# Statistics, powers and normalised rows of two batches in one step, in the two outer stages of a four-layer cross-attention kernel

## The chip, the cores and the metric

The kernel runs on one core of a Trainium2 chip. A core has five engines with their own instruction streams that meet through semaphores: PE (matrix multiply, with its weight load shown as PEld), DVE (vector), ACT (activation), POOL and SP (which issues the DMAs). The metric is the device time of one launch in microseconds.

## The reference, cut to what matters

Eight batches of 128 rows and 256 columns (`x`) and a context of the same shape pass through four layers. Each layer normalises the rows, attends, adds the result and runs an MLP. The normalisation is what the change touches; it is computed 64 times in the outer stages (4 layers' inputs, outputs and MLPs, 8 batches each).

```python
def layer_norm(x, w, b):                      # L0, L2, L3; also ahead of the MLP
    mu = jnp.mean(x, axis=-1, keepdims=True)
    var = jnp.mean(jnp.square(x - mu), axis=-1, keepdims=True)
    return (x - mu) * jax.lax.rsqrt(var + 1e-5) * w + b

def rmsnorm(x, w):                            # L1's MLP
    var = jnp.mean(jnp.square(x), axis=-1, keepdims=True)
    return x * jax.lax.rsqrt(var + 1e-6) * w

x = L0(x, ctx)      # cross-attention to ctx, 16 heads of 16, then MLP
x = L1(ctx, x)      # x attends to ctx and x, masked softmax; rmsnorm ahead of its MLP
x = L2(x, ctx, ctx) # two cross-attentions, 16 heads of 128, with a bias key and value; MLP
x = L3(x, ctx)      # self-attention with a mask, cross-attention with a mask, MLP
# L3: scores = scores * mask - 10000.0 * (1.0 - mask); probs = softmax(scores)
```

## The kernel before

**Streams and stages.** The 8 batches are cut into 4 streams k = 0 to 3 of SB = 2 batches. A row tile has 128 rows on the partitions, 256 columns and two batches, `m.x(k)[:, b, :]`. Stage A computes L0 and L1, stage B the two attentions of L2 (its matmuls split into high and low parts), and stage C L2's MLP (named M2), L3's self-attention (L3s), its cross-attention (L3c) and its MLP. Stage A runs over the span from 0 to about 300 us, stage C from about 820 us to the end. Stage B is a loop and is not touched. There the statistics already have the joint form, with one power for both batches (lines 954 to 959 and L1324).

**The order.** What each outer stage does stands in a text: `ORDER_ONE` (stage A, from line 359) and `ORDER_TWO` (stage C, from line 401). Each of the five engine programs walks the same text and issues its own instructions of each step, in that order. An engine never overtakes itself, so a step's place in the text is its place in every engine's queue. The last number of a step is a PSUM bank where it has one. The steps that matter:

- `stats NAME OF K B`: DVE waits for the rows, then `bn_stats` (L829), `bn_aggr` (L831) and the sum of variance and epsilon, `ve` (L838; for L1's MLP a square and an add, L834 and L836). POOL waits for `ve` and raises it to the power −0.5, `rstd` (L1324). NAME and OF are the layer and which normalisation: `in` ahead of an attention, `mlp` ahead of an MLP, and `L1 out` for the rows that stage B takes.
- `xn NAME OF K B`: the normalised row. For L0 and L1's MLP POOL computes it (L1337, or L1335 without a mean). For the others POOL computes the shift `nb` (L1328) and ACT the row (L1126).
- `turn_in NAME OF K BANK`: PE transposes the normalised rows of both batches (L481). It waits for the row of batch SB − 1, the last.
- `scores`, `minima`, `exp`, `even`, `turn`, `weigh`, `project`: the attention of a unit (a batch of a stream, in halves). PE multiplies (L573), DVE or POOL puts the mask on (L870, L873, L1371), DVE takes the minimum (L880), ACT the exponent (L1198), DVE the sum and its reciprocal (L885, L887), POOL divides (`even`, L1377), PE transposes the weights (L583) and ACT copies them (L1174), PE weighs the values (L598) and projects (L610), and DVE adds to the rows (`project`, L901).
- `residual` (L1360) is POOL's sum of rows and a bias. `up` and `down` are the MLP's two matmuls (L489, L557).

In stage A, the key mask (`m`, L1049) is made by DVE at the first unit's scores. `stats L0 in 0 1` is followed by `parities` on DVE.

In ORDER_TWO before, the last part reads:

```text
turn 15 1, stats L3c mlp 3 0, turn_in L3c mlp 2 7, xn L3c mlp 3 0, weigh 15, up L3c 2 0 4,
project 15 7, stats L3c mlp 3 1, up L3c 2 2 5, xn L3c mlp 3 1, residual L3c mlp 3,
up L3c 2 4 7, turn_in L3c mlp 3 3, up L3c 2 6 4, up L3c 3 0 5, ...
```

Of the kernel before, what the change touches and what calls it, by code (L numbers as in the profile page):

```python
# [18 lines left out]
SB = B // NS  # L19
# [323 lines left out]
class Drains:  # L343
# [24 lines left out]
    xn L0 mlp 1 0, residual L0 mlp 0, up L0 0 6 2, project 3 3, residual L0 attn 3, stats L0 mlp 1 1, turn 4 1, scores 6, minima 6, exp 5 0, even 5 0,
    exp 5 1, weigh 4, down L0 0 0 7, down L0 0 1 2, project 4 5, exp 6 0, exp 6 1, turn_in L1 in 0 0, xn L0 mlp 1 1, turn 5 0, even 5 1, v L0 3 0 1,
    even 6 0, even 6 1, turn_in L0 mlp 1 7, turn 5 1, scores 7, minima 7, k L1 0 1 7, residual L0 mlp 1, weigh 5, turn 6 0, q L1 0 3, stats L0 mlp 2 0,  # L370
    exp 7 0, v L1 0 0 5, even 7 0, project 5 0, turn 6 1, exp 7 1, stats L0 mlp 2 1, xn L0 mlp 2 0, k L1 1 0 7, scores 8, weigh 6, turn 7 0, even 7 1,
    up L0 1 0 0, up L0 1 2 4, xn L0 mlp 2 1, minima 8, up L0 1 4 7, turn 7 1, scores 9, weigh 7, exp 8 0, up L0 1 6 7, even 8 0, minima 9, v L1 0 1 3,
    residual L1 attn 0, turn_in L0 mlp 2 1, project 6 0, exp 8 1, even 8 1, exp 9 0, even 9 0, down L0 1 0 2, stats L0 mlp 3 0, turn 8 0, down L0 1 1 7,
    exp 9 1, even 9 1, turn 8 1, scores 10, weigh 8, turn 9 0, project 7 1, stats L0 mlp 3 1, turn 9 1, minima 10, turn_in L1 in 1 7, exp 10 0, exp 10 1,
    scores 11, residual L0 mlp 2, even 10 0, even 10 1, up L0 2 0 7, up L0 2 2 4, k L1 1 1 0, minima 11, up L0 2 4 2, up L0 2 6 1, exp 11 0, exp 11 1,
# [1331 lines left out]
```

## Time and profile before

| | us |
|---|---|
| median of 3 runs | 1079.56 |
| lowest, highest | 1079.14, 1081.27 |
| the profiled execution, its time | 1081.11 |
| the profiled execution, its span | 1079.80 |

The profiled execution's span is what the rows below are times in; 1.31 us lie around it. The mean granted TensorE clock of the profiled execution is 0.998. Each row is one group of instructions, or a stretch. In a timeline a row has the start, the length, the engine, the line of the kernel, the operation, output and input, and how many instructions it holds; a bracket gives the idle time of the engine before it and what ended it.

### The profile page before, as it was taken

Reading aid. Unit: us, or ns where it says so; the run is one execution under the profiler, and the core shown is the slowest. Engines: PE = TensorE matmul, PEld = TensorE weight load, DVE = VectorE, ACT = ScalarE, POOL = GpSimd, SP = SyncE. Lnnn points to the kernel's source line nnn. Section 1 sums busy time; section 2 is a strip of 40 time slices with the busy share of each in tenths; the row PEclk is TensorE's granted clock in tenths of the full one; section 3 lists DMA queues with packets and bytes.
Section 4 is the critical chain, followed back from the end, with each engine's and each line's share of the span. In section 5 each row is a group of like instructions: output and inputs, shape, how many; then the busy total and the mean of one; then the engine's idle time right before and its main releaser. Section 6 shows DMA issues by size and latency. Waiting matters only on the chain.

```text
span 1079.8 us, 20226 instructions
## 1 busy us (share of the span) xinstructions
PE 1045.6 (97%) x7794; PEld 917.4 (85%) x7794; DVE 706.6 (65%) x1088; ACT 602.2 (56%) x1323; POOL 572.0 (53%) x618
## 2 busy tenths in 40 slices
PE   6899999999999999999999999999999999988999
PEld 5788788788888999999998999999998887866887
DVE  6888778879537556555658655655654377988840
ACT  4998887778653232223334323322226489999972
POOL 7555535455664434333466434443525378999860
PEclk9999999999999999999999999999999999999999
DMA  9200000000113222122120111101100000000000
GB/s 336 112 2 21 2 1 1 2 1 2 49 42 96 70 69 59 40 79 79 40 76 26 40 40 39 40 29 31 31 1 2 1 1 1 2 2 2 10 11 20
DMA packets 33783, 40.66 MB, mean 38 GB/s; under 512 B 2111, under 2 KB 31257, under 8 KB 32025
## 3 DMA queue, kind: packets, MB, share of 16 engines
q1 hardware_dynamic: 33689, 39.38, 11.1%
q8 instruction: 63, 1.03, 0.4%
q14 instruction: 31, 0.25, 0.1%
HBM read 38.32 MB, written 1.05 MB: 36 GB/s over the span
## 4 chain that ended last, share of the span: by engine, by line
PE 77%; POOL 9%; issue 5%; DVE 5%; ACT 4%; DMA 0%; SPq 0%; POOLq 0%; DVEq 0%; ACTq 0%
PE psum L489 14%; PE psum L663 13%; PE psum L557 10%; PE psum L677 7%; PE psum L723 7%; PE psum L583 5%; PE psum L711 5%; PE psum L691 4%; POOL C tile L1371 3%; PE psum L573 3%; PE psum L598 3%; PE psum L700 2%; PE psum L541 2%; PE psum L610 2%; POOL C tile L1377 2%
## 5 line engine op out<-in xcount | busy, mean ns | idle before, releaser
L1459 POOL TENSOR_TENSOR B tile<-B tile,B rec 128x1024 f32<-128x1024 f32 x32 | 60.7, 1897 | 207.8 <-DVE B rec L994 207.8
L1377 POOL TENSOR_TENSOR A tile<-A tile,outer rec 128x1024 f32<-128x1024 f32 x48 | 90.4, 1894 | 99.4 <-DVE outer rec L887 99.4
L1257 ACT ACTIVATE B own<-B max 128x8 f32<-128x8 f32 x32 | 6.7, 210 | 163.1 <-DVE B tile L981 163.1
L1198 ACT ACTIVATE A tile<-A tile,outer min 128x128 f32<-128x128 f32 (+1 forms) x256 | 92.1, 459 | 3.6 <-DVE outer min L880 3.5
L1126 ACT ACTIVATE B kT<-psum,B bcol 128x1024 f32<-128x1024 f32 x32 | 35.6, 1113 | 90.8 <-PE psum L663 90.8
L489 PE MATMUL psum<-A hT,weights 128*128 128x256 f32 x352 | 81.2, 381 | 2.0 <-ACT A hT L1126 2.0
L489 PE MATMUL psum<-C hT,weights 128*128 128x256 f32 x352 | 80.3, 381 | 1.3 <-DVE C tile L870 1.1
L1198 ACT ACTIVATE C tile<-C tile,outer min 128x128 f32<-128x128 f32 x256 | 77.5, 398 | 3.2 <-DVE outer min L880 3.2
L1022 DVE TENSOR_TENSOR x_all<-x_all,psum 128x512 f32<-128x512 f32 x64 | 42.6, 685 | 54.3 <-PE psum L723 54.3
L489 PEld LDWEIGHTS psum<-A hT,weights 128*128 128x128 f32 x352 | 65.2, 190 | 12.5 <-ACT A hT L1126 3.2
L489 PEld LDWEIGHTS psum<-C hT,weights 128*128 128x128 f32 x352 | 65.5, 190 | 11.3 <-issue 2.1
L677 PE MATMUL psum<-B v hi,B cT hi 128*128 128x256 f32 x256 | 74.3, 290 | 0.4 <-ACT B kT L1126 0.3
L677 PE MATMUL psum<-B v hi,B cT lo 128*128 128x256 f32 x256 | 72.4, 283 | 0.0
L677 PE MATMUL psum<-B v lo,B cT hi 128*128 128x256 f32 x256 | 72.4, 283 | 0.0
L802 DVE TENSOR_SCALAR B qT<-psum,B bcol 128x1024 f32<-128x1024 f32 x32 | 41.1, 1283 | 47.3 <-PE psum L663 47.3
L1324 POOL TENSOR_TENSOR outer rstd<-outer ve,half 128x1 f32<-128x1 f32 x64 | 36.0, 565 | 67.5 <-DVE outer ve L838 55.5
L1377 POOL TENSOR_TENSOR C tile<-C tile,outer rec 128x1024 f32<-128x1024 f32 x32 | 60.5, 1897 | 10.6 <-DVE outer rec L887 10.4
L873 DVE TENSOR_TENSOR A tile<-m,psum 128x1024 f32<-128x1024 f32 x48 | 56.4, 1216 | 13.9 <-PE psum L573 13.8
L1174 ACT COPY A PT<-psum 128x512 f32<-128x512 f32 x96 | 51.5, 593 | 24.4 <-PE psum L583 24.3
L711 PEld LDWEIGHTS psum<-B PT,B v 128*128 128x128 f32 x512 | 61.4, 191 | 3.6 <-ACT B PT L1266 1.5
L711 PE MATMUL psum<-B PT,B v 128*128 128x128 f32 x512 | 62.1, 275 | 1.1 <-ACT B PT L1266 1.1
L885 DVE TENSOR_REDUCE outer sum<-A tile 128x4 f32<-128x1024 f32 (+1 forms) x48 | 57.9, 1207 | 7.6 <-ACT A tile L1198 7.5
(197 smaller groups left out, 3113.6 us busy)
## 6 DMA issues: line engine op xcount, KB each, us to landing
weights<-in_weights_c SPq DMA_DIRECT2D x6, 1024.0 KB, 6.9
raw<-in_wq SPq DMA_DIRECT2D x32, 128.0 KB, 2.7
raw<-in_wk SPq DMA_DIRECT2D x32, 128.0 KB, 2.8
raw<-in_wv SPq DMA_DIRECT2D x16, 256.0 KB, 2.7
raw<-in_wo SPq DMA_DIRECT2D x16, 256.0 KB, 2.8
weights<-in_weights_a SPq DMA_DIRECT2D x1, 3072.0 KB, 21.7
weights<-in_weights_a SPq DMA_DIRECT2D x1, 2048.0 KB, 11.3
wide<-in_bias_v SPq DMA_DIRECT2D x2, 1024.0 KB, 10.6
```

Source lines behind the costliest of these rows:

```text
L489: i = pe.matmul(bank(k)[:, n * T:(n + 1) * T], wt[:, c, (o + n) * P:(o + n + 1) * P], src[:, c, :], start=c == 0, stop=c == C - 1)
L557: i = pe.matmul(bank(z)[:, 0:D], part.aT(k)[:, c, b * P:(b + 1) * P], w2[:, c, :], start=c == 0, stop=c == FC - 1)
L583: i = pe.transpose(bank(4 + half)[:, j * P:(j + 1) * P], part.tiles[u % 4][:, q * P:(q + 1) * P], m.ident[:, :])
L663: i = pe.matmul(bank(banks[n]), wt[wp][:, c, :], src[sp][:, c, n * BANK:(n + 1) * BANK], start=(c, wp, sp) == (0, 0, 0), stop=c == C - 1 a ...
L677: i = pe.matmul(bank(z)[:, k * 2 * HK:(k + 1) * 2 * HK], m.bcT[cp][:, c, (2 * n + k) * S:(2 * n + k + 1) * S], m.cut["v"][wp][:, c, :], st ...
L711: i = pe.matmul(bank(z)[:, k * P:(k + 1) * P], m.vv[:, 4 * n + k, h * HK:(h + 1) * HK], m.bPT[:, h, n, k * P:(k + 1) * P], start=True, sto ...
L723: i = pe.matmul(bank(z)[:, k * D:(k + 1) * D], m.bOT[h][op][:, (2 * n + k) * S:(2 * n + k + 1) * S], m.cut["o"][wp][:, h, :], start=(h, op ...
L873: dve.tensor_tensor(tile(u, ly.nk), mask.to_broadcast(shape), sc, ALU.subtract).then_inc(s["masked"].sem, s["masked"].mark((st, u)))
L885: dve.tensor_reduce(part.sum[:, u % 4, 0:ly.per], tile(u, ly.nk), AX.X, ALU.add).then_inc(s["sum_made"].sem, s["sum_made"].mark((st, u)))
L1198: i = act.activation(of_head, of_head, ACT.Exp, bias=part.min[:, u % 4, h:h + 1], scale=-1.0)
L1377: pool.tensor_tensor(tile(u, ly.nk), tile(u, ly.nk), part.rec[:, u % 4, 0:ly.per].unsqueeze(2).to_broadcast([P, ly.per, ly.nk]), ALU.mult) ...
L1459: pool.tensor_tensor(tv, tv, m.brec[:, h, :].unsqueeze(2).to_broadcast([P, B, S]), ALU.mult).then_inc(s["normalised"].sem, s["normalised"] ...
```

## The change

Each stream's two `stats` steps become one `stats NAME OF K`, and its two `xn` steps one. DVE runs both `bn_stats`, both `bn_aggr` and one sum over 128 x 2. POOL raises both columns in one instruction. POOL's `xn` waits once and then makes both rows or both shifts; ACT waits for each shift and makes both rows. The 64 steps of each kind become 32. Signals between the parts are renamed to go with it. PE's waits stay on the last batch's row.

Both orders are rewritten. Every other step, and every bank number, stands in the same sequence as before; a joint step stands where the step of batch 1 stood. The one place where the sequence of joint steps differs is in stage C: before, `xn L3c in 3 0, xn L3c mlp 0 0, xn L3c mlp 0 1, xn L3c in 3 1`, after, `xn L3c mlp 0, xn L3c in 3`.

```diff
 ORDER_ONE
-    stats L0 in 0 0, ctx 0 7, k L0 0 0 7, xn L0 in 0 0, stats L0 in 0 1, xn L0 in 0 1, stats L0 in 1 0, v L0 0 0 2, turn_in L0 in 0 5, stats L0 in 1 1,
-    stats L0 in 2 0, stats L0 in 3 0, stats L0 in 2 1, ctx 2 4, xn L0 in 2 0, q L0 0 0, xn L0 in 2 1, stats L0 in 3 1, ctx 1 7, scores 0, ctx 3 7,
+    ctx 0 7, k L0 0 0 7, stats L0 in 0, xn L0 in 0, v L0 0 0 2, turn_in L0 in 0 5, stats L0 in 1, stats L0 in 2, ctx 2 4, q L0 0 0, xn L0 in 2,
+    stats L0 in 3, ctx 1 7, scores 0, ctx 3 7, k L0 1 0 5, minima 0, residual L0 attn 2, exp 0 0, scores 1, v L0 1 0 5, xn L0 in 1, xn L0 in 3,
...
 ORDER_TWO
-    turn 15 1, stats L3c mlp 3 0, turn_in L3c mlp 2 7, xn L3c mlp 3 0, weigh 15, up L3c 2 0 4, project 15 7, stats L3c mlp 3 1, up L3c 2 2 5,
-    xn L3c mlp 3 1, residual L3c mlp 3, up L3c 2 4 7, turn_in L3c mlp 3 3, up L3c 2 6 4, up L3c 3 0 5, up L3c 3 2 3, up L3c 3 4 5, up L3c 3 6 0,
+    turn_in L3c mlp 2 7, weigh 15, up L3c 2 0 4, project 15 7, stats L3c mlp 3, up L3c 2 2 5, xn L3c mlp 3, residual L3c mlp 3, up L3c 2 4 7,
+    turn_in L3c mlp 3 3, up L3c 2 6 4, up L3c 3 0 5, up L3c 3 2 3, up L3c 3 4 5, up L3c 3 6 0, down L3c 2 0 1, down L3c 2 1 5, down L3c 3 0 7,
...
 DVE
-        def stats(name, of, k, b):
-            event, rms = (name, of, k, b), (name, of) == ("L1", "mlp")
-            x, mean, var = (part.xb[k] if rms else m.x(k))[:, b, :], part.mv[k][:, b, 0:1], part.mv[k][:, b, 1:2]
-            ve = part.ve[k][:, b:b + 1]
+        def stats(name, of, k):
+            event, rms = (name, of, k), (name, of) == ("L1", "mlp")
+            x, mean, var = part.xb[k] if rms else m.x(k), part.mv[k][:, :, 0], part.mv[k][:, :, 1]
+            ve = part.ve[k][:, :]
+            for b in range(SB):
...
+                dve.bn_stats(part.bn[k][:, 6 * b:6 * b + 6], x[:, b, :]).then_inc(s["stats_made"].sem, s["stats_made"].mark((event, b)))
+            for b in range(SB):
+                dve.wait_ge(s["stats_made"].sem, s["stats_made"].at((event, b)))
+                dve.bn_aggr(part.mv[k][:, b, :], part.bn[k][:, 6 * b:6 * b + 6]).then_inc(s["stats_made"].sem, s["stats_made"].mark((event, b, "mv")))
+            dve.wait_ge(s["stats_made"].sem, s["stats_made"].at((event, SB - 1, "mv")))
 ACT
-        def normalise(name, of, k, b):
+        def normalise(name, of, k):
+            rms = (name, of) == ("L1", "mlp")
+            for b in range(SB):
+                rstd = part.rstd[k][:, b:b + 1]
...
+                    act.wait_ge(s["nb_made"].sem, s["nb_made"].at((name, of, k, b)))
+                    i = affine(part.xn[k][:, b, :], m.x(k)[:, b, :], rstd, part.nb[k][:, b:b + 1])
+                i.then_inc(s["xn_act"].sem, s["xn_act"].mark((name, of, k, b)))
 POOL
+        def normalise(name, of, k):
+            pool.wait_ge(s["rstd_made"].sem, s["rstd_made"].at((name, of, k)))
+            for b in range(SB):
...
             if what == "stats":
-                rstd(tuple(a), part.ve[a[2]][:, a[3]:a[3] + 1], part.rstd[a[2]][:, a[3]:a[3] + 1], 1)
+                rstd(tuple(a), part.ve[a[2]][:, :], part.rstd[a[2]][:, :], SB)
...
-                _, _, k, b = a
-                pool.wait_ge(s["rstd_made"].sem, s["rstd_made"].at(tuple(a)))
-                shift(tuple(a), part.mv[k][:, b, 0:1], part.rstd[k], part.nb[k], b)
+                name, of, k = a
+                pool.wait_ge(s["rstd_made"].sem, s["rstd_made"].at((name, of, k)))
+                for b in range(SB):
+                    shift((name, of, k, b), part.mv[k][:, b, 0:1], part.rstd[k], part.nb[k], b)
```

## Rows read from the trace of the kernel before

**Rows 1.** The page's busy time of each engine, its share of the span, and instructions.

```profile
PE 1045.6 (97%) x7794; PEld 917.4 (85%) x7794; DVE 706.6 (65%) x1088; ACT 602.2 (56%) x1323; POOL 572.0 (53%) x618
```

**Rows 2.** Busy time by stretch: its length; PE, PEld, DVE, ACT, POOL; PEclk, DMA, GB/s.

```profile
162.00:189.00 27.00, 27.00 (x209) 22.18 (x209) 23.63 (x37) 20.55 (x45) 15.46 (x11) 1.00 0.00 1
945.00:972.00 27.00, 21.96 (x237) 17.01 (x237) 22.57 (x35) 26.05 (x74) 24.99 (x19) 1.00 0.01 2
```

**Rows 3.** Groups by line, whole span: busy us, mean ns; idle before and releaser.

```profile
L1324 POOL TENSOR_TENSOR outer rstd<-outer ve,half 128x1 f32<-128x1 f32 x64 | 36.0, 565 | 67.5 <-DVE outer ve L838 55.5 <-DVE outer ve L836 11.8
L829 DVE BATCH_NORM_STATS2 outer bn<-x_all 128x6 f32<-128x256 f32 x56 | 23.4, 418 | 4.8 <-DMA x_all<-in_x 4.0
L1328 POOL TENSOR_SCALAR outer nb<-outer mv,outer rstd 128x1 f32<-128x1 f32 x40 | 12.7, 326 | 1.1
L831 DVE BATCH_NORM_AGGREGATE outer mv<-outer bn 128x2 f32<-128x6 f32 x64 | 11.7, 182 | 2.2
L838 DVE TENSOR_SCALAR outer ve<-outer mv 128x1 f32<-128x1 f32 x56 | 8.6, 154 | 1.9
```

**Rows 4.** Timeline of DVE and POOL in stage B, where the joint form stands already.

```profile
564.60 0.75 DVE L954 BATCH_NORM_STATS2 B bn<-x_all 128x6 f32<-128x256 f32 x2
565.60 0.17 DVE L959 TENSOR_SCALAR B ve<-B mv 128x2 f32<-128x2 f32 x1
565.68 0.69 DVE L1022 TENSOR_TENSOR x_all<-x_all,psum 128x512 f32<-128x512 f32 x1
565.85 0.71 POOL L1324 TENSOR_TENSOR B rstd<-B ve,half 128x2 f32<-128x2 f32 x1 [2.28 <-DVE B ve L959]
```

**Rows 5.** Timeline of DVE, POOL and PE in the first 61 us.

```profile
18.51 0.42 DVE L829 BATCH_NORM_STATS2 outer bn<-x_all 128x6 f32<-128x256 f32 x1
54.69 1.22 POOL L1337 TENSOR_SCALAR A xn<-x_all,outer mv,outer rstd 128x256 f32<-128x256 f32 x1
56.18 3.80 POOL L1377 TENSOR_TENSOR A tile<-A tile,outer rec 128x1024 f32<-128x1024 f32 x2 [0.26 <-DVE outer rec L887]
60.04 1.08 PE L583 MATMUL psum<-ident,A tile 128*128 128x128 f32 x8
```

**Rows 6.** Timeline of POOL and PE at 292 us, around L1's output rows.

```profile
292.60 0.93 POOL L1335 TENSOR_SCALAR A xn<-A xb,outer rstd 128x256 f32<-128x256 f32 x1
293.32 1.09 PE L481 MATMUL psum<-ident,A xn 128*128 128x128 f32 x8 [0.33 <-ACT A xn L1126]
```

**Rows 7.** Timeline of ACT and PE around 948 us: L3c's input rows, stream 1.

```profile
948.09 0.60 ACT L1126 ACTIVATE C xn<-x_all,outer nb,outer rstd 128x256 f32<-128x256 f32 x1 [0.16 <-POOL outer nb L1328]
949.21 0.66 PE L481 MATMUL psum<-ident,C xn 128*128 128x128 f32 x4
```

**Rows 8.** Timeline of POOL and PE from 929 to 995 us.

```profile
929.55 1.90 POOL L1377 TENSOR_TENSOR C tile<-C tile,outer rec 128x1024 f32<-128x1024 f32 x1 [0.29 <-DVE outer rec L887]
967.37 1.09 PE L583 MATMUL psum<-ident,C tile 128*128 128x128 f32 x8 [2.27 <-POOL C tile L1377]
980.00 4.67 POOL L1371 TENSOR_TENSOR C tile<-wide,C tile 128x1024 f32<-128x1024 f32 x2 [1.44 <-DVE C tile L870]
992.59 1.90 POOL L1377 TENSOR_TENSOR C tile<-C tile,outer rec 128x1024 f32<-128x1024 f32 x1
```

**Rows 9.** Timeline of the weight loads (PEld) at three of stage C's row transposes.

```profile
824.33 0.42 PEld L481 LDWEIGHTS psum<-ident,C xn 128*128 128x128 f32 x4 [1.49 <-ACT C xn L1126]
872.40 0.42 PEld L481 LDWEIGHTS psum<-ident,C xn 128*128 128x128 f32 x4 [0.26 <-ACT C xn L1126]
910.48 0.42 PEld L481 LDWEIGHTS psum<-ident,C xn 128*128 128x128 f32 x4 [0.16 <-ACT C xn L1126]
```

**Rows 10.** Timeline of POOL, ACT and PEld at 1053 us: the last rows that are normalised.

```profile
1052.27 0.55 POOL L1324 TENSOR_TENSOR outer rstd<-outer ve,half 128x1 f32<-128x1 f32 x1 [4.65 <-DVE outer ve L838]
1053.36 0.60 ACT L1126 ACTIVATE C xn<-x_all,outer nb,outer rstd 128x256 f32<-128x256 f32 x1
1054.00 0.51 PEld L481 LDWEIGHTS psum<-ident,C xn 128*128 128x128 f32 x4
```

More of the change, by code:

```diff
@@ L368 @@
[L368 to L375, printed above, removed]
@@ new lines @@
+    project 23 4, stats L1 mlp 3, xn L1 out 0, down L1 2 1 7, turn_in L1 out 0 5, xn L1 mlp 3, turn_in L1 mlp 3 7, parts 0, keys_of 0, up L1 3 0 7,
+    up L1 3 2 0, up L1 3 4 1, residual L1 mlp 3, stats L1 out 1, up L1 3 6 5, value_bias, stats L1 out 2, values_of 0, xn L1 out 2, down L1 3 0 7,
+    xn L1 out 1, turn_in L1 out 1 4, weights_of 1, down L1 3 1 2, stats L1 out 3, turn_in L1 out 2 1, parts 1, xn L1 out 3, parts 2, keys_of 1,
+    values_of 1, keep 1, turn_in L1 out 3 7, parts 3, values_of 2, keep 0, queries_of 0, keep 2, queries_of 1, keep 3
@@ L414 @@
-    k L3c 3 0 1, stats L3s in 3 0, minima 5, even 4 1, down M2 3 1 3, exp 5 0, turn 4 0, even 5 0, exp 5 1, q L3c 0 7, v L3s 2 0 0, turn 4 1,
-    xn L3s in 3 0, stats L3s in 3 1, xn L3s in 3 1, even 5 1, scores 6, project 2 4, residual L3s attn 3, weigh 4, stats L3c in 1 0, turn_in L3s in 3 0,
-    project 3 1, turn 5 0, turn 5 1, stats L3c in 1 1, minima 6, scores 7, exp 6 0, exp 6 1, even 6 0, even 6 1, minima 7, weigh 5, k L3s 3 0 0,
-    project 4 3, v L3c 2 0 2, exp 7 0, q L3s 3 7, turn 6 0, xn L3c in 1 0, stats L3c in 2 0, xn L3c in 1 1, even 7 0, turn 6 1, exp 7 1, scores 8,
@@ new lines @@
+    output 3, up M2 0 0 2, up M2 0 2 1, xn M2 mlp 1, up M2 0 4 7, residual M2 mlp 2, up M2 0 6 5, turn_in M2 mlp 2 1, residual M2 mlp 0,
+    residual M2 mlp 3, turn_in M2 mlp 1 7, down M2 0 0 5, down M2 0 1 7, up M2 2 0 5, residual L3s attn 0, stats L3s in 0, xn L3s in 0, up M2 1 0 7,
+    up M2 1 2 3, turn_in L3s in 0 5, up M2 1 4 0, k L3s 0 0 4, q L3s 0 5, up M2 2 2 7, stats M2 mlp 3, xn M2 mlp 3, scores 0, up M2 2 4 4, up M2 1 6 5,
+    up M2 2 6 7, scores 1, minima 0, down M2 1 0 7, down M2 1 1 2, exp 0 0, exp 0 1, residual L3s attn 1, stats L3s in 1, xn L3s in 1, minima 1, even 0 0,
@@ new lines @@
+    turn_in M2 mlp 3 0, even 0 1, down M2 2 0 3, exp 1 0, turn_in L3s in 1 1, down M2 2 1 2, even 1 0, exp 1 1, even 1 1, turn 0 0, k L3s 1 0 0,
+    q L3s 1 7, stats L3s in 2, v L3s 0 0 1, turn 0 1, xn L3s in 2, scores 2, weigh 0, turn 1 0, turn_in L3s in 2 7, minima 2, turn 1 1, exp 2 0, scores 3,
+    k L3s 2 0 5, even 2 0, minima 3, weigh 1, exp 2 1, even 2 1, v L3s 1 0 0, exp 3 0, q L3s 2 3, exp 3 1, even 3 0, project 0 1, up M2 3 0 7,
+    up M2 3 2 2, turn 2 0, up M2 3 4 3, project 1 0, up M2 3 6 7, even 3 1, turn 2 1, stats L3c in 0, xn L3c in 0, scores 4, residual L3s attn 2, weigh 2,
@@ new lines @@
+    residual L3c attn 0, turn 3 0, minima 4, turn_in L3c in 0 7, turn 3 1, exp 4 0, scores 5, exp 4 1, weigh 3, even 4 0, down M2 3 0 7, k L3c 3 0 1,
+    minima 5, even 4 1, down M2 3 1 3, exp 5 0, turn 4 0, even 5 0, exp 5 1, q L3c 0 7, v L3s 2 0 0, turn 4 1, stats L3s in 3, xn L3s in 3, even 5 1,
+    scores 6, project 2 4, residual L3s attn 3, weigh 4, turn_in L3s in 3 0, project 3 1, turn 5 0, turn 5 1, stats L3c in 1, minima 6, scores 7, exp 6 0,
+    exp 6 1, even 6 0, even 6 1, minima 7, weigh 5, k L3s 3 0 0, project 4 3, v L3c 2 0 2, exp 7 0, q L3s 3 7, turn 6 0, xn L3c in 1, even 7 0, turn 6 1,
@@ L433 @@
+    turn_in L3c mlp 3 3, up L3c 2 6 4, up L3c 3 0 5, up L3c 3 2 3, up L3c 3 4 5, up L3c 3 6 0, down L3c 2 0 1, down L3c 2 1 5, down L3c 3 0 7,
+    down L3c 3 1 1
 """
```

141 lines of the change are left out of this document (59 added, 82 removed).

## Prediction

> **What bounds the kernel now.** I read the busy times first: PE works 97% of the span, POOL 53% and DVE 65% [rows 1]. Time can only be won or lost where PE stops, or where a delayed input makes it stop. The stretches show where that is: in a middle stretch of stage A PE has no idle time at all, while from 945 to 972 us it is busy 21.96 of 27 us, with ACT at 26.05 and POOL at 24.99 [rows 2]. There three engines form a ring (mask and minimum on DVE, exponent on ACT, mask and division on POOL, transpose on PE) and POOL and ACT are nearly full. The granted clock is 1.00 in both stretches, so no term below comes from the clock.
>
> The groups by line say what a normalisation's statistics cost: 64 small powers on POOL at 565 ns, 36.0 us in all; bn_stats at 418 ns, bn_aggr at 182 ns, the add of eps at 154 ns [rows 3]. Last I read each place where a normalised row feeds PE, for the time between the ready row and PE's first transpose of it. PE always waits for batch 1 of the stream (the wait names the last batch). So the question for each of the 32 merged steps is not what batch 0 cost, but what is added behind batch 1's arrival.
>
> **Where the steps go.** Both orders keep every other step and every bank in the same sequence; a merged step stands where batch 1's step stood (one exception, below). So batch 0's work is taken from an earlier place and put just ahead of, or behind, batch 1's. PE, SP and the DMAs keep their instructions; nothing is moved past a DMA queue.
>
> **DVE, one merged step.** Stage B already has the merged form: two bn_stats begin at 564.60, the joint add begins at 565.60 and the next instruction starts at 565.68 [rows 4]: 1.08 us from start to next start, and 565.60 + 0.17 − 564.60 = 1.17 us from start to the result. Unmerged, one batch is 418 + 182 + 154 ns [rows 3] = 0.75 us, 1.5 us for both. So DVE saves some 0.4 us per stream in all, but at batch 1's place the merged step is 1.08 − 0.75 = 0.33 us longer.
>
> **POOL, one merged step.** The power over two columns takes 0.71 us [rows 4], one column 0.565 [rows 3]. Busy time falls by 64 × 0.565 − 32 × 0.71 = 13.4 us over the kernel, 0.42 per stream; at batch 1's place it is 0.14 longer. Where POOL also normalises (L0, and L1's MLP), the second row comes behind: 1.22 us [rows 5] or 0.93 [rows 6]. Elsewhere POOL only makes the shift, a second one at 0.33 us [rows 3] and ACT normalises a second row at 0.60 us [rows 7].
>
> **Where the saving goes.** A removed early step pays only if its engine was the last to arrive at that moment. In the full stretch POOL's waits are set by DVE: 1.44 us idle before 980.00, 0.29 before 929.55 [rows 8]. A power that is no longer issued there lengthens that wait. In stage A PE has queued work to cover everything. I put the saving at 0 and come back to it as a rival.
>
> **Where the added work is late.** PE's idle time ends at these places, one term each. For the other 21 steps the row is ready well ahead of PE's transpose, by more than is added; what covers them is the queue of PE's own matmuls. The tightest of them is L3c input 1, ready at 948.09 + 0.60 and read at 949.21 [rows 7], 0.52 us; its two rows already stood back to back, so there only 0.14 us of POOL is added. They cost nothing; if their cover were gone, each would cost at most 0.33 + 0.14 + 0.60 = 1.1 us.
> 1. Start, L0 stream 3. DVE's stats at 18.51 [rows 5] are followed by the key mask and then by the first masked scores, the head of the first attention's chain. +0.33 less a little slack: **+0.3** (0 to 0.4).
> 2. L0 MLP of stream 0. POOL's xn of 1.22 us at 54.69 stands ahead of two divisions from 56.18 to 59.98, and PE's transpose starts at 60.04 [rows 5]. The division waited 0.26 us. Added are 1.22 + 0.14, less 0.26, at most 1.1; but PE goes through its own transposes and ACT waits for other things before that division is missed, which takes half or more: **+0.3** (0 to 0.6), the middle.
> 3. L1 output of stream 0 and L1 MLP of stream 3. POOL's 0.93 us row at 292.60 follows a power and a shift, and PE starts at 293.32 after 0.33 us idle on ACT's row [rows 6]; MLP 3's transposes stand right behind. Added: 0.14 + 0.33 + 0.93 = 1.4 less what the transposes ahead cover: **+1.1** (0.5 to 1.5).
> 4. M2 MLP of stream 0, at 824.33, PE loader idle 1.49 us ending on ACT's row [rows 9]. Both batches arrive together here, so one step replaces two back to back: DVE, the power, and then shifts and rows that overlap in pairs: 1.17 + 0.71 + 0.33 + 2 × 0.60 = 3.4 for the merged chain, 1.50 + 0.565 + 0.33 + 0.60 = 3.0 for two batches in a row, with what is between the instructions in both: **+0.1** (0 to 0.4), as the second power of today also waits for the first row's shift.
> 5. L3s stream 1 at 872.40, idle 0.26 [rows 9]: the DVE and POOL part is a little later, ACT's second row partly hidden: **+0.2** (0 to 0.9).
> 6. L3c stream 0 at 910.48, idle 0.16 [rows 9]: **+0.15** (0 to 0.9).
> 7. L3s stream 3. DVE's step lies ahead of the reciprocal that releases POOL at 929.55; POOL then runs on to the division that PE awaits at 967.37 [rows 8], so a delay is passed on: **+0.28** (0 to 0.33).
> 8. L3c stream 2. Its power stands ahead of a division in the same run of POOL work, and PE is idle 2.27 us before 967.37 on it [rows 8]: 0.14 and a little from DVE, **+0.18** (0 to 0.33).
> 9. L3c stream 3. Four shifts, then the division at 992.59 [rows 8]; DVE's 0.33 and POOL's 0.14 in sequence: **+0.48** (0 to 0.6).
> 10. L3c MLP of stream 3, the last. Power at 1052.27, ACT's row at 1053.36, PE's load at 1054.00 [rows 10], and PE works without a gap from there to the end. Added in one chain: DVE 1.17 − 0.75 = 0.42, the wait being for the later batch; POOL 0.14; ACT's second row 0.60 less the part that lies beside the second shift (about 0.3): **+0.87** (0.5 to 1.2).
>
> The exception in the order: L3c MLP 0's rows now go ahead of L3c input 3's. They were two and two around each other; MLP 0 gains about a row, input 3 loses nothing: 0.
>
> Sum: 0.3 + 0.3 + 1.1 + 0.1 + 0.2 + 0.15 + 0.28 + 0.18 + 0.48 + 0.87 = 3.96 us. The lower ends add to 1.0 and the upper ends to 7.2; for this case I keep 2.5 to 5.5, since not all terms fall on one side. The profiled execution took 1081.11 us (span 1079.80, 1.31 around it), so the sum gives 1085.07. The median of the three runs, 1079.56, lies 1.55 below the profiled one: forecast 1083.5, own range 1082.0 to 1085.0.
>
> **Rival 1, no difference.** PE's short waits absorb the ties: a step that ends 0.05 us ahead of PE today may be one whose input PE reached early because its own queue is deep. Then only the terms where PE already stood idle for the same row count: 4, 5, 6 and half of 10, some 0.1 + 0.2 + 0.15 + 0.45 = 0.9, and saving elsewhere gives part of it back: 1080.3. For it: PE at 97% [rows 1]. Against: the ready-to-start distance is near zero at terms 3, 5, 6 and 10, and from 1054.00 PE has no gap in which to make up.
> The Trainium skill (Perfetto Trace Analysis, Identifying Performance Opportunities) says that a kernel gets faster by making its most-contended engine faster. By that rule, as nothing on PE changes, the time stays at 1079.6; the rule says nothing against a loss, and the trace shows PE busy at 97% but waiting in the late stretches.
>
> **Rival 2, faster.** In the stretch from 917 to 1012 us POOL is nearly full (24.99 of 27 us [rows 2]), and six merges lie there, each taking 0.42 us from it. If POOL is what the ring turns by, that is −2.5 us, and the losses 7 to 9 vanish inside it: with the terms of rival 1 for the rest, 0.9 − 2.5 = −1.6: 1078.0. If DVE's 0.40 us per merge lies in series with it, 0.9 − 6 × 0.82 = −4.0: 1075.5. The middle of the two, 1076.8, is this rival's time. It decides once POOL's waits on DVE in that stretch are short beside the powers removed. For it: POOL's share. Against: ACT is fuller (26.05) and loses no work, and POOL's wait of 1.44 us [rows 8] ends on DVE.
>
> **Rival 3, slower still.** The ring passes every added 0.33 + 0.14 us on: a merged step in it delays DVE's next mask, ACT's exponents, POOL's division and PE, and none of it is regained. With six merges in the stretch at 0.48 = 2.9 us in place of terms 7 to 9 (0.94): 3.96 + 1.95 = 5.9 us: 1085.5; with term 3 and 2 at their upper ends (+0.7) 1086.2. It decides if the engines' idle time in the ring is a tie at each merged step and not at three of six.
>
> That the change doesn't do what it says (fewer powers) can be excluded: the code issues one power per stream.
>
> **How the numbers follow.** Forecast 0.55; rival 1 0.20; rival 2 0.14 (0.09 faster, 0.05 the same, as its two prices lie on both sides of the bound); rival 3 0.11. A measurement of this kernel tells 0.2%, 2.2 us, from no change, so faster is below 1077.4 and slower above 1081.7. The forecast's case lies above 1081.7 all but about 0.03. That makes faster 0.09, same 0.28, slower 0.63. The range: down to 1078.8, leaving out the lower part of rival 2, about 0.11, and up to 1086.2, leaving out about 0.07.
>
> **What would show it.** In the profile after: powers 32 × about 0.70 us in place of 64 × 0.565 (POOL busy down by 13 us); DVE busy down by about 10; PE's busy time the same. PE's idle before the L1 output's and L1 MLP 3's transposes grows by about 1 us, the last MLP's first load starts 3.5 to 4 us later than 1054.00, of which 0.9 is its own chain. If the load comes no later than 1054.00 + 1.5, rival 1 holds; if POOL's idle time from 917 to 1012 doesn't rise and PE's falls, rival 2 holds. The prediction is wrong if the steps ahead of the last one have moved PE by less than 2 us in sum, or if the DVE part of merged steps costs other than 1.08 us.

## Result, and the profile of the changed kernel

The changed kernel takes 1090.25 us (median of 5, 1086.15 to 1091.10), the kernel before 1081.27 in the same comparison (median of 5, 1079.14 to 1083.63). The ratio is 1.0075, 95% interval 1.0053 to 1.0097: slower, by 8 to 9 us. The forecast was 1083.5, the range's upper end 1086.2. The direction was right, the size was not. Two disturbed executions of later runs (3717.54 us in e6_three, 1766.19 us in e13_columns_busy) are left out of the medians below.

The page of the changed kernel, its busy time (line numbers after the change lie 3 to 8 below those of before):

```profile
PE 1049.5 (96%) x7794; PEld 920.1 (84%) x7794; DVE 704.4 (65%) x1052; ACT 601.7 (55%) x1323; POOL 559.8 (51%) x586
```

POOL has lost 12.2 us of work and 32 instructions against [rows 1], as forecast (13). DVE was to lose some 10 us and lost 2.2. The groups by line (busy us, mean ns; idle before and releaser) show why:

```profile
L1320 POOL TENSOR_TENSOR outer rstd<-outer ve,half 128x2 f32<-128x2 f32 x32 | 23.3, 728 | 57.2 <-DVE outer ve L832 53.1 <-DVE outer ve L830 3.3
L822 DVE BATCH_NORM_STATS2 outer bn<-x_all 128x6 f32<-128x256 f32 x56 | 20.8, 413 | 4.1 <-DMA x_all<-in_x 4.0
L832 DVE TENSOR_SCALAR outer ve<-outer mv 128x2 f32<-128x2 f32 x28 | 15.9, 568 | 1.0
L825 DVE BATCH_NORM_AGGREGATE outer mv<-outer bn 128x2 f32<-128x6 f32 x64 | 9.6, 173 | 0.0
```

The power is at 728 ns, near the 710 of [rows 4]. But the sum of variance and epsilon takes 568 ns on the mean, where 128x1 took 154 [rows 3] and the same 128x2 form took 0.17 us in stage B [rows 4]. It isn't 568 each time: 19 of the 28 take 0.17, nine take 0.46 to 4.41 us. One of the nine, L3c's input of stream 1, on the timelines of DVE, POOL and PE of the changed kernel:

```profile
937.13 0.74 DVE L822 BATCH_NORM_STATS2 outer bn<-x_all 128x6 f32<-128x256 f32 x2
938.12 1.39 DVE L832 TENSOR_SCALAR outer ve<-outer mv 128x2 f32<-128x2 f32 x1
939.43 2.33 DVE L874 TENSOR_REDUCE outer min<-C tile 128x8 f32<-128x1024 f32 x2
...
934.80 4.68 POOL L1368 TENSOR_TENSOR C tile<-wide,C tile 128x1024 f32<-128x1024 f32 x2
939.44 1.28 POOL L1357 TENSOR_TENSOR raw<-x_all,rows 128x512 f32<-128x512 f32 x1
...
943.04 3.33 PE L481 MATMUL psum<-C hT,weights 128*128 128x256 f32 x8 [1.93 <-DVE C tile L864]
```

POOL's mask instructions end at 934.80 + 4.68 = 939.48. DVE's sum, begun at 938.12, ends at 939.51. Behind it on DVE stand the two minima, then the masks for which PE waits at 943.04. The same place in the kernel before, with POOL in the same mask work until 931.51 + 4.69 = 936.20:

```profile
934.85 0.15 DVE L838 TENSOR_SCALAR outer ve<-outer mv 128x1 f32<-128x1 f32 x1
...
931.51 4.69 POOL L1371 TENSOR_TENSOR C tile<-wide,C tile 128x1024 f32<-128x1024 f32 x2
...
938.73 1.53 PE L489 MATMUL psum<-C hT,weights 128*128 128x256 f32 x6 [0.70 <-DVE C tile L870]
```

There the sum took 0.15 us right beside POOL. In the kernel before 26 of the 56 sums of 128x1 begin while POOL is in an instruction over two large tensors with over 0.2 us to go, and none takes over 0.16 us. In the changed kernel nine of 28 begin so, and all nine end 0.02 to 0.03 us after POOL's instruction. I call such a sum held.

**Where the time comes from.** PE runs the same 7794 instructions in the same order in both kernels, so one can subtract start from start, matmul by matmul. The lag grows in steps. In the changed kernel's profiled execution (span 1089.30, 9.4 us of lag at the end) these steps are, but for some under 0.1 us:

| place in the kernel before | growth of the lag |
|---|---|
| up to 55 us (start and clock) | 0.37 |
| 57.61 and 60.04, L0 MLP 0 | 0.53, of which 0.28 comes back at 62.41 to 63.20 |
| 293.32 to 293.92, L1 output 0 and L1 MLP 3 | 1.17 |
| 317.97, first values of stage B | 0.47 |
| 824.33, M2 MLP 0 | 0.10 |
| 872.40, L3s input 1 | 0.41 |
| 910.48, L3c input 0 | 0.41 |
| 938.73, behind L3c input 1 | 1.23 |
| 939.46 to 940.97, matmuls at half rate | 1.69, of which 0.27 comes back |
| 959.34, behind L3c input 2 | 0.81 |
| 967.37 to 969.26, a wait of 0.15 longer, then matmuls at half rate | 1.79, of which 0.30 comes back |
| 979.97, 991.77 and 994.60, L3c input 3 | 0.72 |
| 1054.15, the last rows | 0.63 |

Rows of the changed kernel (PE, PEld) that answer to [rows 6], [rows 9] and [rows 10]:

```profile
294.58 0.66 PE L473 MATMUL psum<-ident,A xn 128*128 128x128 f32 x4 [1.02 <-ACT A xn L1120]
295.49 0.66 PE L473 MATMUL psum<-ident,A xn 128*128 128x128 f32 x4 [0.25 <-POOL A xn L1332]
...
875.05 0.31 PEld L473 LDWEIGHTS psum<-ident,C xn 128*128 128x128 f32 x3 [0.66 <-ACT C xn L1120]
...
913.55 0.31 PEld L473 LDWEIGHTS psum<-ident,C xn 128*128 128x128 f32 x3 [0.57 <-ACT C xn L1120]
...
1063.50 0.42 PEld L473 LDWEIGHTS psum<-ident,C xn 128*128 128x128 f32 x4 [0.81 <-ACT C xn L1120]
```

Idle time before the transposes has gone from 0.33 to 1.02 + 0.25, from 0.26 to 0.66, from 0.16 to 0.57, and from nothing to 0.81: the places I had named. The last MLP's first load starts at 1063.50, 9.5 us later than 1054.00, where I had expected 3.5 to 4. The second held sum that PE feels, at L3c input 2 (DVE, POOL, PE):

```profile
963.24 0.94 DVE L832 TENSOR_SCALAR outer ve<-outer mv 128x2 f32<-128x2 f32 x1
...
962.87 1.28 POOL L1357 TENSOR_TENSOR raw<-x_all,rows 128x512 f32<-128x512 f32 x1
...
965.89 0.48 PE L481 MATMUL psum<-ctxT_all,weights 128*128 128x256 f32 x1 [0.75 <-DVE x_all L895]
```

And the longest, at L1 output 2, whose DVE had nothing urgent behind it:

```profile
300.24 4.41 DVE L832 TENSOR_SCALAR outer ve<-outer mv 128x2 f32<-128x2 f32 x1
...
300.11 4.52 POOL L1452 TENSOR_TENSOR B bv<-B bv,wide 128x2048 f32<-128x2048 f32 x1
```

### The profile page after: what moved, and what is told of

Same layout as the page of the kernel before. It is cut to its first block, busy times and chain, and to the rows that moved or that the text cites. A ratio compares the mean times of both kernels' runs of the same rounds, so it can differ in the third digit from the quotient of the medians.

```text
span 1089.3 us, 20158 instructions
## 1 busy us (share of the span) xinstructions
PE 1049.5 (96%) x7794; PEld 920.1 (84%) x7794; DVE 704.4 (65%) x1052; ACT 601.7 (55%) x1323; POOL 559.8 (51%) x586
## 4 chain that ended last, share of the span: by engine, by line
PE 77%; POOL 7%; DVE 7%; issue 5%; ACT 3%; DMA 0%; SPq 0%; POOLq 0%; DVEq 0%; ACTq 0%
PE psum L481 14%; PE psum L655 13%; PE psum L549 9%; PE psum L715 7%; PE psum L669 7%; PE psum L575 5%; PE psum L703 4%; PE psum L683 4%; PE psum L590 3%; PE psum L565 3%; PE psum L602 2%; PE psum L533 2%; PE psum L692 2%; POOL C tile L1368 2%; POOL B tile L1457 1%
## 5 line engine op out<-in xcount | busy, mean ns | idle before, releaser
L683 PE MATMUL psum<-B kT,B qT 128*128 128x128 f32 x512 | 62.2, 275 | 0.0
```

Of the source, the lines that this page charges most:

```text
L683: i = pe.matmul(bank(2 * h + b // 4)[:, (b % 4) * S:(b % 4 + 1) * S], m.qT[h][:, b * S:(b + 1) * S], m.kT[h][:, b * S:(b + 1) * S], start= ...
```

## Experiments

Three causes were to be told apart: the **places** (batch 1's rows wait for batch 0's work, my sum), **held sums**, and PE's **clock**. Each was compared with runs of the kernel before on the same chip; those had medians of 1079.45 to 1080.74 us.

**e1_columns.** The changed kernel, the sum per batch (shortened; L1's MLP keeps its joint form):

```diff
-i = dve.tensor_scalar(ve, var, 1e-5, None, ALU.add)        # 128x2
+for b in range(SB):
+    i = dve.tensor_scalar(ve[:, b:b + 1], var[:, b:b + 1], 1e-5, None, ALU.add)
```

> The changed kernel with one edit: the sum of variance and epsilon is made by two 128x1 instructions, one per batch, in place of one of 128x2 (L1's MLP keeps its joint form). Everything else, the joint steps' places, the joint power and both rows behind it, stays. Theory 'held sum': in the trace of the changed kernel 9 of the 28 sums of 128x2 outside L1's MLP take 0.46 to 4.41 us, each beside a POOL instruction, where all 56 sums of 128x1 took 0.15 to 0.16; a sum of 128x1 isn't held. It expects all sums at 0.16 us again, PE's added lag at the changed kernel's 943, 966, 875 and 913 us gone or down to 0.1 to 0.3 us each, and the time 2.5 to 6 us below the changed kernel's (some 1084.5 to 1087.5; more if the two half-rate stretches after the waits go too). Rival 'place': what costs is the second batch's work behind the first's, however it is cut; it expects the time within 1 us of the changed kernel's 1090.25, or slower by 28 x 0.08 us on DVE.

Measured 1085.06 us, ratio to before 1.0044 (1.0028 to 1.0061). Its sums, and PE at the place of 943.04:

```profile
L849 DVE TENSOR_SCALAR outer ve<-outer mv 128x1 f32<-128x1 f32 x56 | 6.0, 149 | 1.0
...
941.19 1.10 PE L494 MATMUL psum<-C hT,weights 128*128 128x256 f32 x4 [0.97 <-DVE C tile L881]
```

All 56 sums are at 149 ns, more instructions in 9.9 us less time, and PE's wait there is 0.97 in place of 1.93. The step at 938.73 in the lag is 0.27 in place of 1.23, that at 959.34 0.09 in place of 0.81. Its profiled execution ends 3.8 us behind before's. Held sums stand, and "place" as the only cause falls.

**e2_place.** As e1_columns, and the power per batch too (two of 128x1 in each step), L1's MLP included.

> The changed kernel's places and steps, but inside each joint step both the sums and the powers are made per batch (128x1, twice). Only the place of batch 0's work differs from the kernel before, and that both bn_stats stand together. 'Held sum': same as e1_columns or up to 1 us slower, since the second power adds 0.42 us of POOL work behind each step (1.1 instead of 0.70). 'Place': within 1 us of the changed kernel, so 1089 to 1092. If the joint power were what gains or loses, this run and e1_columns would lie over 2 us apart.

1087.83 us, ratio 1.0065 (1.0051 to 1.0079): 2.8 us above e1_columns where I expected 1 at most. The joint power is worth something after all: at the places where the chain is late the second power stands in it. The lag's steps are 0.51 in place of 0.26 at L3c input 0, 1.00 in place of 0.47 at 318 us, 0.87 in place of 0.68 at the last rows.

**e3_wide.** The kernel before, order and steps untouched, with the sum over 128x2 (mean and variance of one batch; the power reads its second column):

```diff
-i = dve.tensor_scalar(ve, var, 1e-5, None, ALU.add)                         # 128x1
+i = dve.tensor_scalar(part.vw[k][:, b, :], part.mv[k][:, b, :], 1e-5, None, ALU.add)   # 128x2
```

> The kernel before with one edit: each sum of variance and epsilon is made over 128x2 (mean and variance of one batch, into a tile of its own; the power reads its second column). Order, places and counts are those of the kernel before. 'Held sum': several of the 56 sums take 0.4 to 4.5 us, ending when a POOL instruction ends, and the kernel is 2 to 6 us slower than before. 'Place': no sum beyond 0.2 us, time within 1 us of before.

1088.19 us, ratio 1.0067 (1.0053 to 1.0080). One edit of one operand's width costs the kernel before 7.5 us, above what I expected. Its group, and a held sum with POOL's work beside it:

```profile
L839 DVE TENSOR_SCALAR outer vw<-outer mv 128x2 f32<-128x2 f32 x56 | 35.4, 631 | 1.9
...
934.97 1.28 DVE L839 TENSOR_SCALAR outer vw<-outer mv 128x2 f32<-128x2 f32 x1
...
931.54 4.68 POOL L1372 TENSOR_TENSOR C tile<-wide,C tile 128x1024 f32<-128x1024 f32 x2
```

26 of the 56 sums are held, each until 0.02 to 0.03 us after POOL's instruction (931.54 + 4.68 = 936.22; 934.97 + 1.28 = 936.25). All 26 stand beside POOL instructions over two large tensors. One beside a POOL instruction with a single large source (L0's row, 1.7 us to go) took 0.18. Nine began in the last 0.05 to 0.13 us of a power and took 0.17, too near its end to tell.

**e4_only_c.** The first order as before, the second as changed.

> Steps of two batches in stage C alone (the changed kernel's second order), stage A as in the kernel before. By the lag of PE's instructions in the two profiled executions stage A and the start of B account for 2.2 of 9.4 us, stage C for 7.2. So 5.5 to 7.5 us slower than before if the two parts add; 2 to 3 us slower if the losses in stage C come from the delay that arrives from stage A (a phase, not a cost of its own).

1086.96 us, ratio 1.0056 (1.0042 to 1.0069), 6.3 us above before: stage C has most of the loss by itself, with the same held sums of 1.13, 1.39 and 0.94 us. It isn't a shift inherited from stage A.

**e10_three_sums.** The changed kernel, the sum per batch at L3c inputs 0, 1 and 2 alone.

> The changed kernel with the sum made per batch (two of 128x1) at three of the 28 places, L3c's inputs of streams 0, 1 and 2, whose held sums took 1.13, 1.39 and 0.94 us; the other 25 keep the joint sum, six of them held. If it is these three that lie on PE's path, nearly all of the difference between the changed kernel and e1_columns (5.2 us) is had back: 1085 to 1086.5. If the other held sums (4.41 us at the end of stage A, 1.81 at L3c MLP 0) count, it stays over 1087.5.

1085.86 us, ratio 1.0050 (1.0032 to 1.0068): by the ratios 0.6 us more than e1_columns; the two medians lie 6.4 and 4.4 us above before's on their chips. Of the difference between the changed kernel and e1_columns, three sums bring back 2.7 of 3.3 us by the ratios, and 2.6 of 4.6 by the medians. Of the six that are still held, that of 4.41 us leaves no mark on PE: the lag's step at 318 us is 0.47, as in e1_columns. That of 0.46 us at L3s input 1 adds 0.15; the mark of the other four was not separated.

**e6_three and e11_three_again.** The changed kernel, the joint sum over 128x3 (columns 1 to 3 of mean and variance; the power reads the first and the last).

> The changed kernel with the joint sum made over 128x3 in place of 128x2 (the variance of batch 0, the mean and variance of batch 1; the power reads columns 0 and 2), and nothing else. If being held depends on an even number of columns, no sum is over 0.3 us and the time is that of e1_columns, about 1085. If it depends only on more than one column, source and target being alike, the sums are held as in the changed kernel (9 of 28, the longest 4.4 us) and the time is 1088 to 1091. By the Trainium skill (VectorE: DVE Perf Modes, What auto-detection actually checks) the two-port mode wants the outer sizes of source and target both even, or equal: by that rule the second.

> The same kernel as e6_three (joint sum over 128x3), for a profile that can be set beside the others. Held sums where POOL is in an instruction with two tensors: 5 or more of 28, each ending within 0.05 us of POOL's, if equal outer sizes are enough; none if the number has to be even. Time as e6_three, 1087 to 1090.

e6_three 1087.81 us (three executions; 1088 to 1091 expected), ratio 1.0073 (1.0056 to 1.0090). The same kernel again, e11_three_again: 1088.63 and 1091.62 us, ratio 1.0089 (1.0061 to 1.0118). From its profile, where again nine of 28 are held:

```profile
L850 DVE TENSOR_SCALAR outer vw<-outer mv 128x3 f32<-128x3 f32 x28 | 15.9, 569 | 1.0
...
937.84 1.39 DVE L850 TENSOR_SCALAR outer vw<-outer mv 128x3 f32<-128x3 f32 x1
```

Mean and longest are those of 128x2. An odd number of columns doesn't help; one column does. The Trainium skill (VectorE: DVE Perf Modes, What auto-detection actually checks) has the two-port mode taken when the outer sizes of the single source and the target are both even or equal; that both forms are held, the longest for 4.4 us, agrees. The Trainium skill (SBUF — State Buffer, Who interferes with whom) says that an operation in that mode and a GpSimd operation hold a shared pair of ports in turn, the one that comes later waiting until the first has ended. The nine ends at 0.02 to 0.03 us behind POOL's agree. That a sum of 128x1 isn't held is what the traces show; why a single column isn't was not tried, and no run shows the mode or the ports themselves.

**e7_wait.** The kernel before with 1.3 us of further DVE work at L3c input 1:

```diff
+for again in range(3 if event == ("L3c", "in", 1, 1) else 0):
+    dve.bn_stats(...)          # the same rows again
 dve.bn_stats(...)
```

> The kernel before with three further bn_stats of the same rows at one place, L3c input of stream 1, batch 1 (3 x some 0.42 us = 1.3 us of DVE work, no use of POOL). It imitates the delay of 1.2 us that the held sum makes there. If what a delay at this place costs is the delay and, in some executions, a half-rate stretch of PE's clock behind the wait, then PE's lag at 938.7 grows by 1.2 us and the time by 1.2 to 3 us (1082 to 1084). If held sums did their harm through POOL (which a waiting DVE might block in turn), the cost is 1.3 us or less and no stretch of lower clock appears.

1083.60 us, ratio 1.0033 (1.0021 to 1.0044). The lag grows by 1.19 at 938.73, and then by 1.46 and 1.62 us in two stretches where PE's matmuls take twice as long, behind POOL's divisions at 968 and 989 us; 0.76 comes back between them. A stretch of this kernel (length; PE, PEld, DVE, ACT, POOL; PEclk, DMA, GB/s):

```profile
967.00:979.00 12.00, 10.90 (x132) 8.64 (x132) 9.70 (x19) 9.23 (x26) 10.18 (x9) 0.86 0.01 3
```

and of the changed kernel:

```profile
940.00:948.00 8.00, 6.07 (x51) 4.94 (x48) 7.83 (x10) 6.89 (x22) 6.41 (x5) 0.79 0.01 3
967.00:979.00 12.00, 9.58 (x93) 7.26 (x95) 9.03 (x13) 10.08 (x29) 10.83 (x8) 0.86 0.00 1
```

The granted clock fell to 0.5, which is 1.2 GHz, in parts of these. Before each fall PE had stood idle: 2.27 and 2.02 us ahead of e7_wait's at 968 and 989, 1.93 and 2.42 ahead of the changed kernel's at 943 and 974. The wait alone doesn't decide it: the profile of before has the same 2.27 and 2.02 us without a fall, and e5_chosen's, below, has one at 969 us with its lag at 938.73 grown by 0.27 us only. But the clock is low more often: e7_wait's six executions have a mean granted clock of 0.995 (four) and 0.997 (two), the 19 of before beside it 0.995 once, 0.997 four times and 0.998 else. So a delay of plain work in that place costs more than itself (1.19 us of lag, 2.9 us of the median), with no sum held.

**e9_busy.** The kernel before with work for PE in four of its waits (shortened):

```diff
+if (st, n, r) in {("A", 0, 0), ("A", 0, 1), ("C", 8, 1), ("C", 10, 0)}:
+    claim(4, "weights_drained", (st, u, 0))
+    for j in range(8):
+        pe.transpose(bank(4)[:, ...], m.ident[:, :], m.ident[:, :])
 pe.wait_ge(s["evened"].sem, s["evened"].at((st, u)))
```

> The kernel before, with eight transposes of the identity put into PE's queue ahead of the wait for POOL's division at four places (the first two in stage A, at 30.35 and 33.92 us; 967.37 and 986.58 in stage C, where PE stood idle for 0.36, 2.48, 2.27 and 2.02 us). They write into the bank that the transposes behind the wait fill anew; 0.9 us at full clock each, less than three of the four waits. If the half-rate stretches come of what PE did in the waits, they are shorter or fewer: the mean granted clock goes from 0.998 (0.995 in one run of six) to above it, and the time is 0.5 to 2 us below before. If PE's waits have nothing to do with the clock, 0 to 0.5 us slower than before, since the first place has 0.36 us of wait only.

1079.30 us, ratio 0.9993 (0.9984 to 1.0003). The mean granted clock is 1.000 in all 12 timed executions, where before's 17 beside it have 0.995 to 1.000, five of them 1.000. In its profile:

```profile
27.00:54.00 27.00, 24.97 (x228) 20.88 (x226) 24.62 (x40) 26.07 (x77) 17.36 (x13) 1.00 0.30 113
...
967.00:979.00 12.00, 10.90 (x135) 8.62 (x135) 10.55 (x17) 10.59 (x30) 10.40 (x7) 1.00 0.01 2
```

Before has 0.94 in the first of these stretches, at its first divisions. What PE does in its waits bears on the clock, as expected; the gain of time that I expected (0.5 us or more) can't be told from none, and the spread of the runs is half of before's (2.3 against 4.6 us).

**e12_after_busy, e13_columns_busy, e14_chosen_busy.** The changed kernel, e1_columns and e5_chosen (below), with the transposes of e9_busy and eight more behind unit 5's weighing in stage C.

> The changed kernel with eight identity transposes in PE's queue at five places: the four of e9_busy, and behind unit 5's weighing in stage C, ahead of the wait that grew most (943 us in the changed kernel). If the half-rate stretches are a part of their own of the loss, this kernel keeps clock 1.00 and is 3 to 5 us faster than the changed one: 1085.5 to 1087. If the delays alone made the loss and the clock's part was small, it is less than 2 us faster (over 1088).

> e1_columns (joint steps, the sum per batch) with the same transposes at the same five places. At full clock what is left over e9_busy is what the places cost: by the nine terms that I had summed 3.96 us, by e1_columns' lag 3.8; so 1082.5 to 1083.8. The difference to e12_after_busy is what held sums cost at full clock: by the lag at 875, 913, 943 and 966 us some 2.1 us; if it is under 1 us, held sums do their harm through the clock.

> e5_chosen (23 joint steps, nine left in two parts, the sum per batch) with the same transposes. If POOL's relief is worth anything once the clock is out of it, it is below e9_busy's 1079.3; if the joint steps cost or gain nothing where there is slack, 1078.8 to 1079.8.

On one chip, granted clock 1.000 in all executions counted of the three: 1086.30 us (ratio 1.0049, 1.0036 to 1.0062), 1083.89 (1.0022, 1.0009 to 1.0036) and 1079.98 (0.9995, 0.9984 to 1.0005), before 1080.74. The two stretches of the changed kernel, now in e12_after_busy:

```profile
940.00:948.00 8.00, 7.10 (x44) 6.09 (x36) 7.83 (x9) 8.00 (x26) 6.41 (x4) 1.00 0.00 1
967.00:979.00 12.00, 10.45 (x105) 8.63 (x103) 9.80 (x17) 10.94 (x32) 10.83 (x8) 1.00 0.00 1
```

This divides the loss into three parts: held sums at full clock are e12_after_busy less e13_columns_busy, places e13_columns_busy less e14_chosen_busy, and the rest of the 8.98 us between the medians (8.1 by the ratio) I put down to the clock. The lag column sets the profiled executions start against start, from 39 us on:

| part | by the medians | by the ratios | by the lag | expected |
|---|---|---|---|---|
| held sums | 2.4 | 2.9 | 1.8 | 2.1 |
| places | 3.9 | 2.9 | 3.7 | 3.8 to 4.0 |
| clock, the rest | 2.7 | 2.3 | 2.8 | |

The intervals of the ratios leave each part of the time uncertain by some 2 us; the lag is that of single executions. A further 0.6 us of lag stands between e14_chosen_busy and before. For the held sums the lag shows where they weigh: it grows by 0.15 at L3s input 1, 0.15 at L3c input 0, 0.96 at L3c input 1 and 0.73 at L3c input 2, with 0.2 of small steps back. For the clock, it grows between e12_after_busy and the changed kernel at the two half-rate stretches of stage C; the changed kernel's own five executions go the same way, 1086.15 us at a mean clock of 0.998, 1088.98 at 0.997 and 1090.25 to 1091.10 at 0.994.

**e5_chosen and e8_four.** e1_columns with nine, or four, of the 32 steps put back in two parts at their old places.

> e1_columns (joint steps, but the sum per batch) with nine of the 32 steps put back as they were before, each in two parts at their old places: those where e1_columns' PE lag grew or where I had priced a loss (L0 MLP 0, L1 output 0 and 3, L1 MLP 3, L3s input 1, L3c input 0, 2 and 3, L3c MLP 3). The other 23 stay joint. 'The loss is in what stands behind batch 1 at places without slack': the 3.8 us of e1_columns' lag vanish, time within 1 us of before, 1079.5 to 1082. If the relief of POOL (23 powers of 0.42 us) is worth anything in stage C, it shows here alone: up to 2.4 us below before. Rival 'joint steps cost wherever they are' (more work at once on DVE and POOL): 2.7 us above before still, since 23 of 32 stay.

> e1_columns with four of the 32 steps put back in two parts at their old places: L1 output 0 and 3, L1 MLP 3, and L3c MLP 3 (the last). In e1_columns' trace PE's lag grows by 1.12 us at the first two's transposes, 0.52 at the start of stage B's values, and 0.62 at the last. If each of these costs is its own, this kernel is 2.3 us faster than e1_columns (about 1082.8); if they only hand on delays that come back elsewhere, less than 1 us faster.

e5_chosen: 1081.11 us, ratio 1.0005 (0.9995 to 1.0015). The loss is in these nine places and 23 joint steps cost nothing that the time shows; nor do they gain: neither this nor e14_chosen_busy is measurably faster than before, and the latter's 1079.98 us lies 0.2 above the 1078.8 to 1079.8 that I expected. e8_four: 1084.15, ratio 1.0034 (1.0022 to 1.0046), 0.9 us below e1_columns where 2.3 were expected. In its profile the four places did give back what they cost in e1_columns': 1.15 us at L1 output 0 and L1 MLP 3, 0.46 at the start of stage B, 0.68 at the last rows. But the clock fell twice, behind 968 and 989 us, where it didn't in e1_columns' profile. The two medians mix executions with and without such falls, and so say less than e5_chosen's.

## Why the prediction was right in direction and wrong in size

**Places: right in sum, 3.96 us forecast, 3.9 measured (2.9 by the ratios).** Term by term, by the steps of the lag between before and e13_columns_busy:

| term | forecast | measured |
|---|---|---|
| 1, start | 0.3 | no loss found |
| 2, L0 MLP 0 | 0.3 | 0.65, of which 0.28 comes back by 63.20 |
| 3, L1 output 0 and MLP 3 | 1.1 | 1.17 |
| not priced: L1 output 3, at 318 us | 0 | 0.47 |
| 4, M2 MLP 0 | 0.1 | 0.14 |
| 5, L3s input 1 | 0.2 | 0.26 |
| 6, L3c input 0 | 0.15 | 0.26 |
| 7 and 8, to L3c input 2 | 0.46 | 0.38, of which 0.27 at 938.73 |
| 9, L3c input 3 | 0.48 | 0.52 |
| 10, the last | 0.87 | 0.68 |
| not priced: a gain at 181.77 us | 0 | −0.07 |

The measured column adds to 4.2. That the sum fits so well is in part luck: the start that I had priced cost nothing, and a place that I had not priced cost more. L1 output 3 was among the 21 steps that I called covered: ACT's second row ends 0.49 us later there than the lag around it accounts for, ahead of the first key copy of stage B, and PE waits for that copy. The 0.27 at 938.73 stands behind L3c input 1, the tightest of those I called covered, and may be its own; no run separates it from term 7. So "what covers them is the queue of PE's own matmuls" was right for 19 or 20 of 21.

**DVE, one merged step: the step that failed.** I took 1.17 us from stage B [rows 4] and wrote that the prediction would be wrong "if the DVE part of merged steps costs other than 1.08 us". It did: from the first `bn_stats` to the end of the sum it took 1.16 to 5.41 us, 1.56 on the mean of 28, where I had 1.17. The row I read the price from had a bracket that told it: POOL was idle for 2.28 us, waiting for that very sum. It was a price for an idle POOL, and I used it in a stretch that I had myself called nearly full of POOL work [rows 2]. The bound for an operation that the trace of before doesn't show in this company should have been taken from below and above: 0.17 us, and the length of a POOL instruction (1.90 us for a division, 2.36 for a mask, 4.5 for stage B's bias).

The trace of before did show DVE held by POOL, which I had overlooked. The square and the add ahead of L1's MLP have two tensor inputs each; five of these 16 instructions took 0.34 to 1.76 us and the other eleven 0.16. The five end 0.01 to 0.02 us after a POOL instruction, as here in the kernel before (178.15 + 1.89 = 180.04, 178.63 + 1.42 = 180.05):

```profile
178.63 1.42 DVE L834 TENSOR_TENSOR outer ve<-outer mv 128x1 f32<-128x1 f32 x1
...
178.15 1.89 POOL L1377 TENSOR_TENSOR A tile<-A tile,outer rec 128x1024 f32<-128x1024 f32 x1 [4.13 <-DVE outer rec L887]
```

So one column doesn't keep every DVE operation free: it kept the sum free, which reads one tensor. The Trainium skill (SBUF — State Buffer, Who interferes with whom) had the rule for the sum; I weighed another.

**"No term comes from the clock": failed too.** The granted clock of 1.00 from 945 to 972 us was that of a kernel whose waits ended in time. It had a wait of 2.27 us in that stretch [rows 8]. The changed kernel's profiled execution had two falls in stage C behind longer waits (e7_wait shows two with plain work), and the clock's part is 2.3 to 2.8 us. Before isn't free of it either: 11 of the 65 executions beside the runs have a mean granted clock of 0.995 and take 1082.75 to 1083.73 us. So the forecast needed a term for the clock with a chance on it, not a 0.

**The saving at 0: right.** POOL lost 12.2 us and nothing came of it in e5_chosen. Rival 2 falls, and with it the thought that POOL is what the ring turns by. It needs a limit: the joint power does gain, 2.8 us between e2_place and e1_columns (2.3 by the ratios), but only against two powers at the same late place. Rival 1 falls: the ties were real, and of the ten terms only the start's was absorbed. Rival 3 had its time nearest to the result, for another reason; the ring didn't pass on 0.48 at each of six merges.

What stays open: why one column keeps the sum free, what besides a wait makes the clock fall, and why the start of stage A varied by some 1 us between profiles with the same first instructions.

## What to carry to other kernels

An operation that is made wider to save instructions may begin to wait for another engine: price it beside that engine's work, not where that engine is idle, and look in the trace for operations whose length varies at one form. Join two small steps only where the second one's consumer has slack of its own; the earlier half of the pair was free where it stood. And where PE already waits for 2 us at a time, a microsecond of delay ahead of it can cost two or three, because the clock goes too.

## What the runs showed of the hardware that I had not expected

- A `tensor_scalar` of two or three columns on DVE waits for the end of a POOL instruction over two tensors: 0.17 us alone, 0.46 to 4.41 us beside one, ending 0.02 to 0.03 us after it. With one column it takes 0.15 us in the same company (26 of 26 in the kernel before).
- A DVE operation with two tensor inputs waits for POOL at one column too: in the kernel before five of 16 took 0.34 to 1.76 us, ending 0.01 to 0.02 us after a POOL instruction (four divisions, one cast), the others 0.16.
- Eight transposes of the identity in each of four waits kept the granted clock at 1.000 in 12 of 12 executions; the kernel before had 0.995 to 1.000.
- Two columns in place of one cost the power 0.16 us (565 against 728 ns), so a second power of its own costs three and a half times what a second column does.
